# Adding up W's transposed sums in PSUM, with all eight units of the first pass ahead of step 0

## The reference

```python
w = weights[subjects]                                  # 32 batches, weights[.] is 128 x 128
x1 = jnp.einsum('bct,bcd->bdt', x, w)                  # x: 32 x 128 x 2048
result = jnp.einsum('bnd,od->bno', x1, W_base) + b_base      # W_base: 2048 x 2048
probs = softmax(jnp.einsum('bnd,ed->bne', x1, W_gate))       # 8 experts, the best 2, renormed to route_w
h = jnp.einsum('bnd,erd->bner', x1, A)                       # rank 16
delta = jnp.einsum('bner,eor->bno', h * route_w[..., None], B)
out = x + result + delta * 1.0
```

## Time and profile before

| | us |
|---|---|
| median of three executions | 1632.52 |
| the profiled execution, its own time | 1634.34 |
| its span | 1632.6 |
| opening, to the first product | 0 to 65.65 |
| products of step 0 with s = 0, and units 4 to 7 | 65.65 to 136.89 |
| steady steps | 136.89 to 792.22, 865.68 to the end |
| second pass, units 8 to 15 | 792.22 to 865.68 |

### The profile page before, as it was taken

The page is one execution under the profiler, slowest core; times in us unless marked ns, Lnnn a source line. Parts: engine busy times, 40 slices in busy tenths (PEclk is TensorE's granted clock), DMA queues, the critical chain, the costliest instruction groups (busy, mean ns, idle before and its releaser), DMA issues.

```text
span 1632.6 us, 25730 instructions
## 1 busy us (share of the span) xinstructions
PE 1536.8 (94%) x9539; PEld 837.8 (51%) x9539; DVE 1300.2 (80%) x2228; ACT 596.5 (37%) x996; POOL 631.9 (39%) x473
## 2 busy tenths in 40 slices
PE   5667999999999999999668999999999999999998
PEld 5444555555555555555464555555555555555553
DVE  6666888888888888888776888888888888888874
ACT  6654333333333333333583323333322333332231
POOL 2534455555555555555453122222212221221222
PEclk8788999999999999999889999999999999999999
DMA  5332444444444444444731344343334434333432
GB/s 198 130 117 82 128 136 136 135 135 134 128 136 136 136 127 133 132 134 125 235 104 39 98 137 136 110 122 121 102 91 136 136 113 121 122 105 88 134 107 71
DMA packets 102911, 201.87 MB, mean 124 GB/s; under 512 B 10874, under 2 KB 24186, under 8 KB 102266
## 3 DMA queue, kind: packets, MB, share of 16 engines
q1 hardware_dynamic: 102786, 200.22, 39.8%
HBM read 128.96 MB, written 71.22 MB: 123 GB/s over the span
## 4 chain that ended last, share of the span: by engine, by line
PE 89%; DVE 5%; ACT 2%; issue 2%; DMA 1%; POOL 1%; POOLq 0%; SPq 0%; DVEq 0%; ACTq 0%
PE bank_x L1121 10%; PE bank_x L1122 10%; PE bank_x L1123 10%; PE bank_y L1123 10%; PE bank_y L1122 10%; PE bank_y L1121 10%; PE bank_z L1121 3%; PE bank_z L1123 3%; PE bank_z L1122 3%; PE bank_h L1122 3%; PE bank_h L1121 3%; PE bank_h L1123 3%; PE bank_c L1121 2%; PE bank_c L1123 2%; PE bank_c L1122 2%
## 5 line engine op out<-in xcount | busy, mean ns | idle before, releaser
L475 POOL TENSOR_TENSOR x_res<-x_res,t_sums 128x512 f32<-128x512 f32 x256 | 350.7, 1372 | 895.6 <-DVE t_sums L827 735.5
L1121 PE MATMUL bank_x<-TT,s_parts 128*128 128x512 f16 x768 | 295.5, 385 | 14.8 <-POOL TT L450 7.5
L1122 PE MATMUL bank_x<-TT,s_parts 128*128 128x512 f16 x768 | 295.0, 384 | 0.0
L1123 PE MATMUL bank_x<-TT,s_parts 128*128 128x512 f16 x768 | 294.6, 384 | 0.0
L1121 PE MATMUL bank_y<-TT,s_parts 128*128 128x512 f16 x768 | 291.2, 379 | 0.0
L1122 PE MATMUL bank_y<-TT,s_parts 128*128 128x512 f16 x768 | 291.1, 379 | 0.0
L1123 PE MATMUL bank_y<-TT,s_parts 128*128 128x512 f16 x768 | 291.1, 379 | 0.0
L571 ACT ACTIVATE p_copies<-bank_x,y_inv 128x512 f32<-128x512 f32 x128 | 87.8, 686 | 492.8 <-PE bank_x L1123 398.7
L827 DVE TENSOR_TENSOR t_sums<-t_sums,inv_w 128x512 f32<-128x512 f32 x256 | 218.6, 854 | 8.8
L800 DVE TENSOR_TENSOR s_parts<-a_full,s_parts 128x512 f16<-128x512 f32 x224 | 208.1, 951 | 7.5 <-ACT s_parts L556 7.5
L456 POOL TENSOR_TENSOR x_res<-x_res,BT 128x512 f32<-128x512 f32 x128 | 197.8, 1545 | 4.8 <-DMA x_res<-in_x_dram 3.3
(11 more groups left out here) (219 smaller groups left out, 2715.6 us busy)
## 6 DMA issues: line engine op xcount, KB each, us to landing
x<-in_x_dram SPq DMA_DIRECT2D x32, 1024.0 KB, 5.7
x_res<-in_x_dram SPq DMA_DIRECT2D x128, 256.0 KB, 3.7
part_scratch<-x_res SPq DMA_DIRECT2D x128, 256.0 KB, 2.9
x_res<-part_scratch SPq DMA_DIRECT2D x128, 256.0 KB, 3.9
out_dram<-x_res SPq DMA_DIRECT2D x128, 256.0 KB, 2.8
x_parts<-in_L_ffn_W_base_dram SPq DMA_DIRECT2D x12, 512.0 KB, 5.3
a_full<-in_L_ffn_W_base_dram SPq DMA_DIRECT2D x12, 512.0 KB, 4.8
w_cond<-in_L_cond_weights_dram SPq DMA_DIRECT2D x64, 64.0 KB, 3.9
```

What stands on the lines that cost most here:

```text
L475: nc.gpsimd.tensor_tensor(XR[:, xr_slot(m), :], XR[:, xr_slot(m), :], TM[:, m % 2, :], ALU.add).then_inc(r_added, 1)
L1121: nc.tensor.matmul(dst, lhs[0], rhs[0], start=start, stop=False, skip_group_check=chained)
L1122: nc.tensor.matmul(dst, lhs[0], rhs[1], start=False, stop=False, skip_group_check=chained)
L1123: return nc.tensor.matmul(dst, lhs[1], rhs[0], start=False, stop=stop, skip_group_check=chained)
```

## The change

Each of the four sums is now built by TensorE in the bank of PSUM where its predecessor lies. Two chains of banks per unit: B11, then T1, T2, T4 in one (`ROOT`), and B22, then T3, in the other, which B21 opens afresh (`SIDE`). A stage is one `w_quad` added to what the bank holds, then ACT's upper part and DVE's lower part, and only after the lower part has been read may the next quad be added. For a negative term the diagonal with the minus sign (`minus_diag`) is the moving operand. That makes seven quads, seven upper and seven lower parts per unit; C12's copy, the four sums on DVE and POOL's `w_lower` are gone.

The stages of two units are interleaved. PE, ACT and DVE all follow this order (`w_period(g)`): B11(g), B22(g), T2(g-1), B21(g-1), T1(g), T4(g-1), T3(g); PE has `spread(g)` after T2(g-1), and ACT takes its result (`w_inverse(g)`) ahead of B11(g). The first unit has `w_begin`, the last `w_end`.

POOL makes the diagonals (`w_diagonals`: six 128x128 operations per unit). The absolute sum of one block stays on ACT, that of the other goes to DVE. The rows of a unit lie in one of six areas; in the second pass they are three (`PARTS`, `FULL`, `COPIES`), and unit g takes the place of unit g-3.

In the first pass all eight units come ahead of product(0, 0, 0); the seven products with s = 0 then follow each other, and the finishing of their tiles (`copy_p`, `finish`, `add_r`) moves behind the units as well.

```diff
+        AREA = [RESIDUAL, BIAS, COPIES, RESIDUAL, PARTS, FREE, FULL, PARTS,
+                PARTS, FULL, COPIES, PARTS, FULL, COPIES, PARTS, FULL]
...
# SP, first pass
+            sp.wait_ge(w_tr, n_stage(4, T4))
+            load_rows(7)
+            sp.wait_ge(w_tr, n_stage(5, T4))
+            load_tile(4)
+            load_tile(5)
...
# SP, second pass
+                    sp.wait_ge(r_added, 8 * NP)
+                    load_rows(NU + 2)
...
-                    for g in range(NU + 2, 2 * NU):
-                        sp.wait_ge(w_tr, 4 * (g - 1))
+                    for g in range(NU + 3, 2 * NU):
+                        sp.wait_ge(w_tr, n_stage(g - 3, T4))
                         load_rows(g)
...
# POOL
+            def w_diagonals(g):
+                pool.wait_ge(w_scaled, g + 1)
+                if g > 1:
+                    pool.wait_ge(w_tr, n_stage(g - 2, T4))
+                for i in range(2):
+                    ins = nc.gpsimd.tensor_scalar(diag[g % 2][:, i, :], ident[:, :], row_rpow2[:, g % 2, i:i + 1], TOP_W,
+                                                  ALU.mult, ALU.mult)
+                ins.then_inc(w_diag, 1)
+                if g > 0:
+                    pool.wait_ge(w_spread, g)
...
             split_f_lo(0, FT[:, :, :, :])
             split_f_lo(1, FT_second)
+            w_diagonals(4)
             pool.wait_ge(bias_in, 16)
+            add_bias(0)
+            w_diagonals(5)
...
# ACT
+            def w_period(g):
+                w_inverse(g)
+                w_upper(g, B11)
+                w_upper(g, B22)
+                w_upper(g - 1, T2)
+                w_upper(g - 1, B21)
+                w_upper(g, T1)
+                w_upper(g - 1, T4)
+                w_upper(g, T3)
...
             sum_rows(2)
+            w_period(1)
             act.wait_ge(agb_spread, 1)
...
                     sum_rows(NU)
+                    sum_rows(NU + 1)
+                    w_begin(NU)
+                    for g in range(NU + 1, 2 * NU):
                         if g + 1 < 2 * NU:
                             sum_rows(g + 1)
-                        w_upper(g)
+                        w_period(g)
+                    w_end(2 * NU - 1)
...
# DVE
             def w_scales(g):
+                dve.wait_ge(rows_in[AREA[g]][1], row_turn(g))
+                link(nc.vector.tensor_reduce(row_sum[:, g % 2, 1:2], rows_of(g, 1), AX_XY, ALU.add,
+                                             apply_absolute_value=True))
                 dve.wait_ge(w_sums, g + 1)
...
             find_maxima(1)
             w_scales(4)
+            find_top(1)
+            w_scales(5)
+            scale_x(1)
+            w_begin(4)
+            w_scales(6)
+            w_period(5)
...
# PE
+                if q == B11:
+                    pe.wait_ge(w_diag, g + 1)
+                    if g - 2 >= begin:
+                        pe.wait_ge(w_lo, n_stage(g - 2, T4))
...
+                elif q == T1:
+                    pe.wait_ge(w_minus, g + 1)
+                    pe.wait_ge(w_lo, n_stage(g, B11))
...
+                elif q == T2:
+                    pe.wait_ge(w_lo, n_stage(g, T1))
...
+                else:
+                    pe.wait_ge(w_lo, n_stage(g, T2))
...
+            def w_period(g):
+                w_quad(g, B11)
+                w_quad(g, B22)
+                w_quad(g - 1, T2)
+                spread(g)
+                w_quad(g - 1, B21)
+                w_quad(g, T1)
+                w_quad(g - 1, T4)
+                w_quad(g, T3)
```

More of the change, by code:

```diff
@@ L186, in adaln_ffn_kernel @@
         wc_in = sem("wc_in")
-        stage_in = [sem(f"stage{i}_in") for i in range(4)]
+        rows_in = [[sem(f"rows{a}_{i}_in") for i in range(2)] for a in range(6)]
         a_in = sem("a_in")
@@ L483, in _ @@
             part.then_inc(b_reordered, 1)
-            for g in range(4):
-                w_lower(g)
+            for g in range(1, NU // 2):
+                w_diagonals(g)
             pool.wait_ge(a_copied, 4)
@@ L643, in _ @@
             sum_rows(3)
-            w_upper(2)
+            w_period(2)
             copy_features(2)
@@ new lines, in w_begin, with w_end @@
+            def w_begin(g):
+                w_lower(g, B11)
+                w_lower(g, B22)
+                w_lower(g, T1)
+                w_lower(g, T3)
+            def w_period(g):
+                w_lower(g, B11)
+                w_lower(g, B22)
+                w_lower(g - 1, T2)
+                w_lower(g - 1, B21)
+                w_lower(g, T1)
+                w_lower(g - 1, T4)
+                w_lower(g, T3)
+            def w_end(g):
+                w_lower(g, T2)
+                w_lower(g, B21)
+                w_lower(g, T4)
@@ L1000, in _ @@
             sum_s2(0)
-            w_sums_and_lower(3)
+            w_period(3)
+            w_end(3)
             agb_scales(2)
@@ L1112, in _ @@
                     w_scales(NU)
-                    for g in range(NU, 2 * NU):
+                    w_scales(NU + 1)
+                    w_begin(NU)
+                    for g in range(NU + 1, 2 * NU):
                         if g + 1 < 2 * NU:
                             w_scales(g + 1)
-                        w_sums_and_lower(g)
+                        w_period(g)
+                    w_end(2 * NU - 1)
         @block.tensor
@@ L1160, in cond, with w_end @@
+            def w_end(g):
+                w_quad(g, T2)
+                w_quad(g, B21)
+                w_quad(g, T4)
             def cond(n, u):
@@ L1268, in transpose_b @@
                 mm.then_inc(b_tr, 1)
-            w_quads(0)
+            w_quad(0, B11)
+            w_quad(0, B22)
             transpose_maxima(0)
+            spread(0)
+            w_quad(0, T1)
+            w_quad(0, T3)
             spread_maxima(0)
             transpose_b(0)
-            w_quads(1)
+            w_period(1)
             transpose_b(1)
@@ L1290, in _ @@
             transpose_a(3)
-            w_quads(3)
+            w_period(3)
+            w_end(3)
             cond(0, U_A12)
@@ L1301, in _ @@
             nc.tensor.matmul(BD[:, 0:P], ones[:, :], agb_diag_inv[:, 0:P], start=True, stop=True).then_inc(agb_spread, 1)
-            pe.wait_ge(w_lo, 3 * (NU // 2))
-            pe.wait_ge(w_sum_lo, 4 * (NU // 2))
+            transpose_maxima(1)
+            pe.wait_ge(w_lo, n_stage(NU // 2 - 1, T4))
             pe.wait_ge(a_copied, 4)
+            w_quad(4, B11)
+            spread_maxima(1)
+            w_quad(4, B22)
+            spread(4)
+            w_quad(4, T1)
+            w_quad(4, T3)
+            w_period(5)
+            w_period(6)
+            w_period(7)
+            w_end(7)
+            pe.wait_ge(w_lo, n_stage(NU - 1, T4))
+            pe.wait_ge(w_inv, NU)
             product(0, 0, 0)
```

383 lines of the change are left out of this document (170 added, 213 removed).

## The result

| | us | ratio to before |
|---|---|---|
| before, median of four executions | 1632.64 (1632.2 to 1633.35) | |
| after, median of four | 1658.55 (1657.57 to 1662.84) | 1.0163 [1.0145, 1.0182] |
| after once more, unedited (an experiment below) | 1658.25 (1656.86 to 1660.87) | 1.0156 [1.0139, 1.0173] |

The forecast was 1651.0 with a range of 1640 to 1664: the sign, the mechanism and the wide range held, the middle was 7.5 us too low, and the time lies 1.5 us beyond the narrower 1644 to 1657 that went with the forecast itself.

What follows compares the result with a forecast made beforehand. PE is busy 94%, so only the opening with the first pass and the second pass can change. Second pass +12.7 and first pass +5.8 make +18.5 on 1634.34, 1652.8; the median lies 1.8 below, 1651.0 us, range 1640 to 1664.

Steps and rivals of the forecast that it cites:

- A loaded period: Second pass, units 11 to 15: rows are asked for late, the load takes 5.3 us, each of five periods 10.1 us.
- Second pass, start and end: After POOL's add at 799.06, B11(8) starts at 801.6 and T4(8) ends at 816.1; whole second pass +12.7 us.
- The end part: End of the second pass: T3, T2, T4 with the parts between and after them, 5.7 us.
- The first pass: From the opening through units 4 to 7 and the s = 0 products, with a clock gain at s = 1: +5.8 us.
- Units 4 to 7: First pass: cover of POOL's split and DVE's maxima gone; B11(4) at 84.9, s = 1 products at 145.2, +8.3 us.
- The opening: Start of first pass: w_period(1) ahead of agb's spread and transpose_a(0); gate's transposes reach 70.3, +4.7 us, bounds 0 and +8.
- POOL's diagonals: POOL's scaled 128x128 diagonals: 0.3 us each; the rival that POOL binds at 1.16 each: 1671 us, 5%.
- The inverse: Period without a load: ACT copies the inverse first, which waits for the spread, so B11's upper part is late: 0.64 us.
- The idle times lower the clock too: Rival, loaded periods: idle about 2.5 us, then T1 and T4 take 1.8 each, period 11.6; 1660 us, 18%.
- Rows in time: Rival: loads as if 3 us or less instead of 5.3, six periods of 8.4, 10 less; 1641 us, 14%.
- Faster: Rival: neither load nor spread binds, the period is VectorE's own 6.0 us, 32 less; 1619 us, 9%.

Runs made afterwards that it cites:

- second run: The changed kernel (after) run once more, unedited, with its own profile: 1658.25 us, ratio 1.0156 to before.
- the inverse late: After, with ACT copying the inverse diagonals behind the upper parts of B11 and B22, in both passes: 1648.56 us, ratio 1.0088 to before.
- the interleaved opening: After, with T1(1), T4(0), T3(1) behind the gate's spread, transpose_a(0), the first cond and transpose_a(1): 1661.82 us, ratio 1.0176 to before.
- the four-area kernel: After, with W's rows in four areas instead of three in the second pass, so loads are issued a period earlier: 1652.83 us, ratio 1.0112 to before.
- the filler kernel: After, with nine matmuls of 512 columns into an unread bank behind B21 in the loaded periods: 1660.19 us, ratio 1.0164 to before.

## Why the prediction was right, and where its sizes were off

- **A loaded period, 10.1 us:** 10.0 in the second run, 10.6 in the first, with the half clock. That rows are asked for too late was shown by taking the wait away: 8.58, forecast 8.4.
- **Second pass, start and end.** B11(8) starts 2.9 us after POOL's add, forecast 2.5; T4(8) ends 18.9 after it, forecast 17.0. That is more than the 1.5 that is missing, and the loaded periods gave 0.4 back. The end part took 5.77, forecast 5.7. The whole is +16.7 to the product's start, forecast +15.2, and 2.0 come back from the clock, forecast 2.5: +14.7 in all, forecast +12.7. The first pass has +10.5, forecast +5.8, and so most of the miss.
- **Units 4 to 7.** The claim that the order removes the cover of POOL's split and DVE's maxima was shown from both sides, by putting the products back (first pass +0.7) and by moving the units alone (+11.3). B11(4) came at 84.78, forecast 84.9. The failed step is the clock behind it: four quads from T1(4) on that I had at full clock for the most part ran at half, and T1(4) itself came 0.6 later (92.0, forecast 91.4), so T4(4) ended at 103.6, not 100.0. The loaded period took 11.7, not 10.1, with T1(6) and T4(5) at half clock after 2.8 us of idleness and the second block there 5.7 us after the issue, not 5.3; in the second run it took 11.3, with 2.2 and 5.1 us. That is 5.2 of the 5.5 us by which s = 1 starts too late (150.70, forecast 145.2).
- **The opening:** agb's spread came at 69.53 and ended at 69.76, forecast 70.3. B11(4) follows the gate's transposes at 16.3 us in the second run, with the inverse late and in the interleaved opening (68.67 to 84.99, 65.64 to 81.95, 71.13 to 87.47), so this term counts in full.
- **POOL's diagonals:** 0.37 to 0.41 us each for the most part, taken as 0.3. In the periods they end no wait of PE; only B11(4) and B11(8), with which the passes begin, wait for them.
- **The inverse,** 0.64 in the forecast's period, was worth 1.2: it delays four upper parts, not one. It was the term to look at: no run shows a cost of moving it.
- **The two rules weighed.** In the second run the block sums waited until 4.0 and 5.2 us after the issue of a pair of loads. The Trainium skill (DMA: Bandwidth & Descriptors, Anatomy of one DMA) gives an estimated 4.4 for the bytes of both, which lies between; by it the period would be an estimated 9.2, and the trace says 10.0. The page's fit is for one transfer on GpSimd's path, and these are two from SyncE. PE fell to half clock behind some idle gaps of 1.9 to 2.8 us and stayed at full behind others. The Trainium skill's rule on gaps between bursts (TensorE: Matmul & The Clock Gate, Why this matters for your kernels) speaks of longer gaps than these, so it agrees with the second kind alone and lends the rival of the lower clock no support.
- **Rivals.** "The idle times lower the clock too" was given 18% at 1660 and came true in part: one loaded period in six in the second run, four in the first, five with the inverse late. That the time came within 2 us of its 1660 is luck: it reckoned with six periods of 11.6, and of after's none took that long but one of 11.7. I had set 2.5 us nearer to the full clock by one row, and left out that the first pass of the kernel before has a case of each kind, full clock after 2.51 us and half clock after 2.06 (below). "Rows in time" is the four-area kernel in the second pass, 1652.8 in place of 1641, mostly since the first pass loses 11 where this rival had some 4. "Faster" was possible only with more edits: 1623 in place of 1619, with PE and not VectorE as the bound.

PE in the first pass of the kernel before:

```profile
117.52 1.16 PE L1150 MATMUL bank_x<-hw,a_full 128*128 128x128 f32 x8 [2.51 <-ACT s_parts L598]
120.73 2.08 PE L1150 MATMUL bank_d<-hw,a_full 128*128 128x128 f32 x8 [2.06 <-DVE TT L936]
```

Open: why the clock falls after some gaps of 1.9 to 2.8 us and not after others, and why the second block landed 5.1 us after the issue in some periods and up to 6.0 in others (the filler kernel's first pass).

## What to carry to other kernels

Moving adds from VectorE into TensorE's accumulation makes a chain of stages, each with three handovers; before counting what it frees, write down which load waits for the end of that chain, and give it one more buffer. Work that looks out of order in a prologue may be the cover of another engine's latency: ask what each engine does meanwhile before it is moved. And two waits in one period hide each other: a loaded period of the second pass lost 1.4 us by the rows in time, nothing by the late inverse alone, and 2.6 by both. Before a small gain is called small, look whether the clock was the same: the late inverse's 1.0 us in the second pass is an estimated 4.7 at an equal clock.

## Unexpected on the hardware

- After an idle time of 2.5 us the first quad behind it was at full clock (1.13 us) and a later one at half (1.91 us), so that the gap and its price stand apart in the profile. In the earlier trace rows an idle time of 2.31 was followed by full clock throughout. Between the two profiled executions of after this made up 2.5 of 3.3 us. It isn't the whole of the spread: the four-area kernel, whose periods have no such gaps, still spreads by 4 us, the kernel before by 2.4 at most.
- With matmuls into an unread bank in the gap, PE ran at 2.4 GHz in all six loaded periods of the one profiled execution, and its four times lie within 0.8 us; nothing was saved, as a transfer ends the wait.
